# Next batch's loads issued by ScalarE, hand-written lists for the closing rounds, late weights first on SyncE

## The reference, cut to what matters

```python
q = layernorm(x) @ Wq ; k, v = split(layernorm(ctx) @ Wkv)       # ln weights and biases left out
q = q * (1 + scale) + shift
x = x + tanh(g_xattn) * (softmax(q k^T / 8) v) @ Wout
h = gelu(bitlinear(layernorm(x), w1, b1))      # int8 rounding of the rows, ternary weights
x = x + tanh(g_ffn) * bitlinear(h, w2, b2)
```

## Time and profile before

| | us |
|---|---|
| median of 3 runs | 1146.59 (1146.12 to 1147.98) |
| the profiled execution, its own time | 1148.09 |
| its span, first to last instruction | 1146.2 |
| TensorE busy | 1069.4 (93%) |
| ScalarE busy | 974.0 (85%) |
| VectorE busy | 943.3 (82%) |
| GpSimd busy | 776.7 (68%) |
| mean granted TensorE clock | 0.978 of full |

### The profile page before, as it was taken

One profiled execution on the slowest core, in us unless ns is written; L12 is line 12 of the kernel. 1 busy time (PEld: TensorE's weight loads), 2 busy tenths in 40 slices (PEclk: granted clock), 3 DMA queues, 4 the chain that ended last, 5 costly groups with the idle time before them and its releaser, 6 DMA issues.

```text
span 1146.2 us, 32095 instructions
## 1 busy us (share of the span) xinstructions
PE 1069.4 (93%) x11890; PEld 735.4 (64%) x11890; DVE 943.3 (82%) x2108; ACT 974.0 (85%) x1866; POOL 776.7 (68%) x837
## 2 busy tenths in 40 slices
PE   3788999999999999999999999999999999999972
PEld 1455666776676676767666676776677667766650
DVE  3686788888889888888888878888988878988863
ACT  4677789999999979999999979999999979998861
POOL 3466577776767777676777666767777776777631
PEclk9899999999999999999999999999999999999975
DMA  8155745676786656778865776676667676755451
GB/s 273 50 97 91 115 87 108 125 114 113 117 137 108 103 113 124 117 108 125 119 111 110 127 115 104 112 136 101 111 126 114 117 122 111 120 107 103 105 103 30
DMA packets 418840, 129.72 MB, mean 113 GB/s; under 512 B 392480, under 2 KB 417536, under 8 KB 418688
## 3 DMA queue, kind: packets, MB, share of 16 engines
q1 hardware_dynamic: 418688, 127.68, 63.5%
HBM read 26.71 MB, written 3.67 MB: 27 GB/s over the span
## 4 chain that ended last, share of the span: by engine, by line
PE 71%; ACT 9%; DMA 6%; issue 6%; POOL 3%; DVE 3%; POOLq 1%; SPq 0%; DVEq 0%; ACTq 0%
PE work L757 15%; PE work L759 14%; PE work L758 14%; PE ps_s L776 10%; DMA pt<-pn 6%; PE ps_o L757 3%; PE ps_o L759 3%; PE ps_o L758 3%; ACT prob L538 2%; PE work L839 2%; PE work L857 2%; ACT L538 2%; ACT q_f L504 2%; PE work L863 2%; PE work L830 2%
## 5 line engine op out<-in xcount | busy, mean ns | idle before, releaser
L379 POOL TENSOR_TENSOR pn<-prob,pn 112x750 f16<-112x750 f32 x256 | 399.5, 1566 | 123.1 <-ACT pn L548 111.6
L538 ACT ACTIVATE prob<-ps_s,neg_max 112x375 f32<-112x375 f32 x512 | 265.2, 573 | 16.7 <-DVE neg_max L680 13.6
L680 DVE TENSOR_REDUCE neg_max<-ps_s 112x2 f32<-112x750 f32 x256 | 237.4, 928 | 23.6 <-PE ps_s L776 23.5
L757 PE MATMUL ps_o<-v_h,pt 128*128 128x65 f16 (+1 forms) x1536 | 168.3, 195 | 18.3 <-DMA pt<-pn 14.6
L757 PE MATMUL work<-z,wkv_h 128*128 128x375 f16 x512 | 168.6, 329 | 15.2 <-DVE k_l L605 8.1
L461 ACT ACTIVATE k_h<-work 128x375 f16<-128x375 f32 x256 | 121.4, 487 | 61.2 <-PE work L759 55.6
L605 DVE SCALAR_TENSOR_TENSOR k_l<-work,k_h 128x375 f16<-128x375 f32 x256 | 136.3, 540 | 40.7 <-ACT k_h L461 40.5
L758 PE MATMUL ps_o<-v_l,pt 128*128 128x65 f16 (+1 forms) x1536 | 168.0, 193 | 0.0
L759 PE MATMUL ps_o<-v_h,pt 128*128 128x65 f16 (+1 forms) x1536 | 168.0, 194 | 0.0
L759 PE MATMUL work<-z,wkv_l 128*128 128x375 f16 x512 | 167.4, 327 | 0.0
L758 PE MATMUL work<-z,wkv_h 128*128 128x375 f16 x512 | 167.0, 326 | 0.0
(11 more groups left out here) (125 smaller groups left out, 2729.7 us busy)
## 6 DMA issues: line engine op xcount, KB each, us to landing
ctx_in<-in_ctx SPq DMA_DIRECT2D x32, 375.0 KB
pt<-pn SPq DMA_TRANSPOSE x256, 3.5
x_in<-in_x SPq DMA_DIRECT2D x32, 112.0 KB, 3.4
x_res<-in_x SPq DMA_DIRECT2D x28, 128.0 KB, 4.1
out<-y SPq DMA_DIRECT2D x28, 128.0 KB, 2.0
stage<-in_wkv SPq DMA_DIRECT2D x2, 1024.0 KB, 9.6
stage<-in_w SPq DMA_DIRECT2D x2, 1024.0 KB, 11.8
stage<-in_wq SPq DMA_DIRECT2D x1, 1024.0 KB, 9.1
```

Of the source, the lines that this page charges most:

```text
L379: g.tensor_tensor(buf[:, 1, :, 0:SK], prob[:, p % 2], buf[:, 0, :, 0:SK], ALU.subtract).then_inc(p_lo, 1)
L538: i = a.activation(prob[:, p % 2, h, :], ps_s[0:SQ, 2 * (p % 2) + h, 0:SK], ACT.Exp, bias=neg_max[:, 2 * (p % 2) + h:2 * (p % 2) + h + 1])
L680: v.tensor_reduce(neg_max[:, 2 * (p % 2):2 * (p % 2) + 2], ps_s[0:SQ, 2 * (p % 2):2 * (p % 2) + 2, 0:SK], X, ALU.max, negate=True).then_in ...
L757: t_.matmul(dst, sh, mh, start=(n == 0), stop=False)
```

## The change

Four edits. ScalarE issues the loads of the next batch's context and queries right behind `LNW`, after a wait for its own last `LNW` instruction; `LD` and `LX` leave SyncE. The late weights are issued by SyncE at once, ahead of its list. `FIRST` is rewritten for all engines, and a third list, `LAST`, is added for the closing rounds (batches 30 and 31 with tiles 24 to 27). For the last tile, the two DMA transposes become TensorE transposes into PSUM (`XT`, `HT`), from which `XTE` and `HTE` clip. The steady lists of TensorE, ScalarE, VectorE and GpSimd stay as they were. In the lists a tile step carries the number of a batch: 31 is tile 27, 30 is tile 26, 29 is tile 25, 28 is tile 24.

```diff
+LAST["PE"] = [
...
+    ("A3", 31), ("F0", 29), ("WO", 30), ("OO0", 31), ("A4", 31), ("A5", 31), ("A6", 31), ("F2", 28),
+    ("A7", 31), ("OO1", 31), ("F0", 30), ("F1", 30), ("WO", 31), ("F2", 29), ("XT", 31), ("F1", 31),
+    ("F0", 31), ("F2", 30), ("HT", 31), ("F2", 31),
+]
 FIRST["ACT"] = [
+    ("LNW", 0), ("WKH", 0), ("ZF0", 0), ("ZF1", 0), ("WQH", 0), ("KH0", 0), ("WVH", 0), ("WOH", 0),
+    ("KH1", 0), ("KH2", 0), ("ZXF", 0), ("LNW", 1), ("KH3", 0), ("TNH", 0), ("QF0", 0), ("ZF0", 1),
...
+LAST["ACT"] = [
...
+    ("OH1", 30), ("E6", 31), ("PH6", 31), ("VH12", 31), ("E7", 31), ("GE", 29), ("SQ", 29), ("XR", 30),
+    ("OH0", 31), ("OH1", 31), ("HR", 29), ("GE", 30), ("SQ", 30), ("XR", 31), ("HR", 30), ("GE", 31),
 FIRST["DVE"] = [
+    ("BA", 0), ("BB", 0), ("BS", 0), ("WKL", 0), ("BA", 1), ("BB", 1), ("BS", 1), ("WQL", 0),
+    ("KL0", 0), ("WVL", 0), ("KL1", 0), ("KL2", 0), ("AS1", 0), ("KL3", 0), ("AS0", 0), ("KL4", 0),
...
+LAST["DVE"] = [
...
+    ("N0", 31), ("PH5", 31), ("OT1", 30), ("VL11", 31), ("M7", 31), ("N1", 31), ("HE0", 29), ("PH7", 31),
+    ("VL12", 31), ("X1", 30), ("XST", 30), ("N2", 31), ("SC1", 30), ("HTE", 28), ("HMX", 29), ("YE", 28),
+    ("OT0", 31), ("N3", 31), ("SC2", 29), ("XTE", 30), ("OT1", 31), ("HE0", 30), ("HE1", 30), ("X1", 31),
+    ("XST", 31), ("HTE", 29), ("HMX", 30), ("SC1", 31), ("YE", 29), ("SC2", 30), ("XTE", 31), ("HE1", 31),
+    ("HE0", 31), ("HTE", 30), ("HMX", 31), ("YE", 30), ("SC2", 31), ("HTE", 31), ("YE", 31),
+]
 ORDER["SP"] = [
-    ("LX", 4), ("T4", 1), ("T5", 1), ("T6", 1), ("ST", -2), ("T7", 1), ("T0", 2), ("XD", 0),
-    ("HD", -1), ("T1", 2), ("LD", 5), ("T2", 2), ("RS", 1), ("T3", 2),
+    ("T4", 1), ("T5", 1), ("T6", 1), ("ST", -2), ("T7", 1), ("T0", 2), ("XD", 0), ("HD", -1),
+    ("T1", 2), ("T2", 2), ("RS", 1), ("T3", 2),
 ]
-            def load(b):
...
+            def load_late_weights():
+                sp.dma_start(gates[:, 0:1], g_x.partition_broadcast(P)).then_inc(small_in, 16)
...
+            load_late_weights()
             for name, b in sequence("SP"):
...
+            for t in (ident, ident_h):
+                i = g.affine_select(out=t[:], in_=t[:], compare_op=ALU.not_equal, fill=1.0, base=0,
+                                    pattern=[[-1, P]], channel_multiplier=1)
...
                     a.activation(x_n[:], x_in[:], ACT.Identity, bias=ln_nb[0:SQ, TT:TT + 1],
                                  scale=ln_rs[0:SQ, TT:TT + 1]).then_inc(ctx_normed, 1)
+                    if b + 1 < B:
+                        act.wait_ge(ctx_normed, b + 1)
+                        act.dma_start(ctx_in[:], ctx[b + 1].rearrange("(t p) d -> p t d", p=TP)).then_inc(ctx_loaded, 16)
+                        act.dma_start(x_in[:], x[b + 1]).then_inc(x_loaded, 16)
...
+                if name == "XTE" and b == NT - 1:
+                    dve.wait_ge(full[BANK["XT", b]], USE["XT", b])
+                    v.tensor_scalar(xqt[:].rearrange("p c q -> p (c q)"), work[:, BANK["XT", b], :].bitcast(F16)[:, 0:KC * P],
+                                    -QMAX - 1, QMAX, ALU.max, ALU.min).then_inc(evacuated[BANK["XT", b]], 1)
...
+                if name == "HT":
+                    pe.wait_ge(hq_ready, b + 1)
+                    for c in range(FF // P):
+                        i = t_.transpose(wh[:, c * P:(c + 1) * P], hid_q[:, c * P:(c + 1) * P], ident_h[:])
```

More of the change, by code:

```diff
@@ L33 @@
 CAST_ACT = (0, 2, 4, 6)
-ORDER, FIRST = {}, {}
+ORDER, FIRST, LAST = {}, {}, {}
 ORDER["PE"] = [
@@ L115 @@
 FIRST["POOL"] = [
[5 rows of a table removed]
[5 rows of a table added]
+]
+LAST["POOL"] = [
[6 rows of a table added]
 ]
 ORDER["SP"] = [
-    ("LX", 4), ("T4", 1), ("T5", 1), ("T6", 1), ("ST", -2), ("T7", 1), ("T0", 2), ("XD", 0),
-    ("HD", -1), ("T1", 2), ("LD", 5), ("T2", 2), ("RS", 1), ("T3", 2),
+    ("T4", 1), ("T5", 1), ("T6", 1), ("ST", -2), ("T7", 1), ("T0", 2), ("XD", 0), ("HD", -1),
+    ("T1", 2), ("T2", 2), ("RS", 1), ("T3", 2),
 ]
 FIRST["SP"] = [
[6 rows of a table removed]
-]
-START, END = -5, B + 4
[4 rows of a table added]
+]
+LAST["SP"] = [
[5 rows of a table added]
+]
+START, END = -2, B + 4
 TOKEN_STEPS = ("WO", "XT", "HT", "F0", "F1", "F2", "XR", "GE", "SQ", "HR", "X1", "XST", "SC1", "XTE", "HE0", "HE1", "HMX", "SC2",
@@ L139, in sequence @@
 def sequence(engine):
-    done = set(FIRST[engine])
+    done = set(FIRST[engine] + LAST[engine])
     steps = FIRST[engine] + [(name, it + off) for it in range(START, END) for name, off in ORDER[engine]
-                             if 0 <= it + off < B and (name, it + off) not in done]
+                             if 0 <= it + off < B and (name, it + off) not in done] + LAST[engine]
     return [(name, b - b // 8 - 1 if name in TOKEN_STEPS else b) for name, b in steps if b % 8 or name not in TOKEN_STEPS]
@@ L328, in _ @@
                     turn(b, int(name[1]))
-                if name == "XD":
+                if name == "XD" and b < NT - 1:
                     turn_quantised(b)
-                if name == "HD":
+                if name == "HD" and b < NT - 1:
                     turn_hidden(b)
-                if name == "LD":
-                    load(b)
-                if name == "LX" and b > 0:
-                    sp.wait_ge(ctx_normed, b)
-                    sp.dma_start(x_in[:], x[b]).then_inc(x_loaded, 16)
                 if name == "RS":
@@ L350, in _ @@
             g.memset(ident[:], 0.0)
+            g.memset(ident_h[:], 0.0)
             g.memset(ln_mv[:], 1.0)
@@ L353, in _ @@
             pool.drain()
-            g.affine_select(out=ident[:], in_=ident[:], compare_op=ALU.not_equal, fill=1.0, base=0,
-                            pattern=[[-1, P]], channel_multiplier=1).then_inc(consts_ready, 1)
+            for t in (ident, ident_h):
+                i = g.affine_select(out=t[:], in_=t[:], compare_op=ALU.not_equal, fill=1.0, base=0,
+                                    pattern=[[-1, P]], channel_multiplier=1)
+            i.then_inc(consts_ready, 1)
             g.memset(v_h[:, :, :, DH:VW], 1.0)
@@ L719, in step @@
                     scales(x1_rms, b, amax1, x1_c, clip1, inv1, qs1, deq1, 0)
-                if name == "XTE":
+                if name == "XTE" and b == NT - 1:
+                    dve.wait_ge(full[BANK["XT", b]], USE["XT", b])
+                    v.tensor_scalar(xqt[:].rearrange("p c q -> p (c q)"), work[:, BANK["XT", b], :].bitcast(F16)[:, 0:KC * P],
+                                    -QMAX - 1, QMAX, ALU.max, ALU.min).then_inc(evacuated[BANK["XT", b]], 1)
+                if name == "HTE" and b == NT - 1:
+                    dve.wait_ge(full[BANK["HT", b]], USE["HT", b])
+                    v.tensor_scalar(hqt[:].rearrange("p c q -> p (c q)"), work[:, BANK["HT", b], :].bitcast(F16)[:, 0:FF // P * P],
+                                    -QMAX - 1, QMAX, ALU.max, ALU.min).then_inc(evacuated[BANK["HT", b]], 1)
+                if name == "XTE" and b < NT - 1:
                     dve.wait_ge(x_turned, 16 * (b + 1))
                     v.tensor_scalar(xqt[:], xqt_r[:], -QMAX - 1, QMAX, ALU.max, ALU.min).then_inc(x_clipped, 1)
-                if name == "HTE":
+                if name == "HTE" and b < NT - 1:
                     dve.wait_ge(h_turned, 16 * (b + 1))
@@ L798, in job @@
                 w = work[:, bank, :]
+                wh = w.bitcast(F16)
                 if USE[name, b] > 1:
@@ L850, in job @@
                                         for c in range(IC)])
+                if name == "XT":
+                    pe.wait_ge(xq_ready, b + 1)
+                    for c in range(KC):
+                        i = t_.transpose(wh[:, c * P:(c + 1) * P], xq[:, c * P:(c + 1) * P], ident_h[:])
+                if name == "HT":
+                    pe.wait_ge(hq_ready, b + 1)
+                    for c in range(FF // P):
+                        i = t_.transpose(wh[:, c * P:(c + 1) * P], hid_q[:, c * P:(c + 1) * P], ident_h[:])
                 if name in ("F0", "F1"):
@@ L853, in job @@
                         pe.wait_ge(tern_ready[0], 1)
-                    pe.wait_ge(x_clipped, b + 1)
+                    if b == NT - 1:
+                        results(b, ["XT"])
+                    else:
+                        pe.wait_ge(x_clipped, b + 1)
                     c = slice(int(name[1]) * HALF, (int(name[1]) + 1) * HALF)
@@ L860, in job @@
                         pe.wait_ge(tern_ready[1], 1)
-                    pe.wait_ge(h_clipped, b + 1)
+                    if b == NT - 1:
+                        results(b, ["HT"])
+                    else:
+                        pe.wait_ge(h_clipped, b + 1)
                     for c in range(FF // P):
```

20 lines of the change are left out of this document (7 added, 13 removed), and 116 rows, old and new, of the table CAST_ACT.

## The result

The changed kernel takes 1151.95 us (median of 12 runs, 1148.72 to 1154.65); beside it the kernel before took 1147.35 us (12 runs, 1146.12 to 1148.55). The ratio is 1.0038, with a 95% interval of 1.0027 to 1.005: slower, by 4.6 us between the medians, where 14 us less were forecast. The time lies inside the forecast range, and the sign is wrong.

A forecast was written before the change was run, and what follows sets the result against it. TensorE was taken to bound the steady part, with most winnable time at the two ends. 1148.09 us with -6 opening, -12 closing and +4 steady gave 1134.1, or 1132.6 as a median; range 1120 to 1172.

The forecast's parts named there:

- Late weights earlier cost SyncE nothing: Opening: issuing the late weights earlier is free for SyncE, as its first transpose is at 52 us.
- I expect it landed between 18 and 25 us: Opening: the second load, issued by ScalarE near 14 us, lands at 18 to 25 us; opening term -6 us.
- Rival B: Opening gains nothing: loads share the engines with early late weights, landing near 25 us; 1138.6 us; chance 0.14.
- I take 6 us in all: Steady part: gain from transposes of pairs 2 and 3 issued sooner, 6 us, bounds 0 and 9.
- Rounds without a tile have more room: Steady part: rounds without a tile absorb ScalarE's hold more easily; added cost put at 27 x 0.37 = 10 us.
- Rival C: Steady part: ScalarE's issues cost 0.7 to 1.4 us more a round, uncovered; 1145 to 1172 us; chance 0.18.
- A: Whole run: the opening, steady and closing terms add without competing; 1132.6 us, bounds 1120 to 1143; chance 0.48.
- Rival D: Steady part: ScalarE's issues wait for SyncE's transpose issues, 2.5 to 5.1 us a round; 1193 to 1266 us; chance 0.20.
- (b): Closing, after the last `WO`: `XR` and `XQ` no longer behind `HR` and `HQ` of tile 26; 0.3 and 0.6 us.
- (c): Closing: from `XQ`'s end to the clip, two TensorE transposes and a PSUM read replace DMA; 1.5 us won.
- (d): Closing: eight TensorE transposes and a PSUM clip replace the last DMA transpose and its clip; 1.1 us won.
- (a): Closing: tile 26's `HMX` no longer between tile 27's `X1` and `XST`, nor `SC2` before `SC1`; 1.2 and 1.0 us.

The follow-up runs named there:

- E4: Not a run: a code step in ScalarE's list, queued behind the two load issues in the changed kernel; it started 0.09 us after `x_n` ended in the kernel before.
- act_context_alone: The kernel before with only the context's load issued by ScalarE behind its layernorm, SyncE keeping the queries' load: 1144.98 us, ratio 0.9975.
- E5: Not a run: a code step in ScalarE's list, for which TensorE waits before `S7` in rounds without `F0` and `F1`.
- The three issues: The kernel before with both loads issued by ScalarE behind `LNW`, plus a third issue loading the queries into an unread spare tile: 1176.67 us, ratio 1.0254.

## Why the prediction was right or wrong

**The opening: wrong, by its own step.** The steps that failed are "Late weights earlier cost SyncE nothing" and "I expect it landed between 18 and 25 us". SyncE indeed lost nothing. The bytes did: the late weights were in flight beside the second context and made it land at 30.06. That this is the cause, and not the second queue or the new lists, two runs show together: the same issues without the early weights gained 4 to 6 us, and the changed kernel with one wait before the weights took 9.6 less. (The weights first in the kernel before lost 2.2 in the median, but mostly because the context was issued 8 us later.) Rival B named this mechanism, and its sign (a second statistics step after 25 us) is in the trace, but it stopped at "gives nothing"; with the statistics and three weight steps queued behind the load, the price went 1.7 us past nothing. The page that speaks for B (the Trainium skill, DMA: Bandwidth & Descriptors, Issuing engines are not separate DMA queues) says that loads issued by different engines interleave on the same 16 engines. The trace agrees: a queue of its own didn't bring the context in sooner, 16.4 us beside the weights and 8.6 with the weights behind, where on SyncE's queue and ahead of the weights it had taken at most 8.5 (issued at 13.54, read at 22.04).

**The steady part: mechanism right, both terms mis-sized.** Place, waits and releasers came as written: `E4` 1.07 us after `x_n` (forecast 1.0), pair 2's transpose issued 0.03 us after GpSimd (0.99 before), and `KL3`, then `F1`, late.

- What is gained was put at 6 us; `act_context_alone` measured 2.0, within the noise of such a part, with 3.3 of the 5.1 us of wait gone. The step that failed is "I take 6 us in all": it summed the waits as if each microsecond of wait were one of time, and its own sentence, that "The weight loads' wait for `QF` partly takes its place", had been given no share. That row was 7.8 us in the steady stretch and is 11.8 after. In the changed kernel TensorE still waits 4.6 us for transposes over the whole run (14.6 before). The transposes do come sooner, but not by what SyncE's waits and long issues had promised. For pair 2 (medians of batches 4 to 29) the wait and the issue fell from 0.99 and 3.75 us to 0.03 and 1.51, but from the issue's end to landing it took 5.46 instead of 3.24. From its start to landing it is 7.0 in both kernels, and in both a context's load is in flight beside it; only the wait was won. From GpSimd's end to landing pair 2 went from 8.1 to 7.0 us, pair 3 from 8.95 to 8.5 and pair 4 from 6.05 to 4.1.
- What is added was put at 27 x 0.37 = 10 us. By the prediction's own numbers 1.1 - 0.67 is 0.43, and 27 x 0.43 is 11.6. The hold grew by 1.07 + 0.09 = 1.16, less 0.67 is 0.49, and the usual round grew by 0.56. So the mechanism was right there, and nearly the size. The step that failed is "Rounds without a tile have more room": the nine rounds in which a tile's step is missing grew by 6.3 us together, 0.7 each, because TensorE waits there for ScalarE itself (`S7` for `E5`, `Z1` behind `QF`) and has no slack of 0.67. With 7.7 in the fifteen usual rounds and -0.7 in the first two that is the 13.3 measured. The three issues agree: the usual round grew again by at least the hold.

**Rival C** had part of this: a cost of ScalarE beyond the slack. Its price was 0.7 to 1.4 a round more than A; the rows show 0.2 more in the usual round and 0.3 more in the short ones. Its mechanism, longer issues, didn't come: the median issues (0.27 and 0.63) held through the steady part. (28 x 0.7 on top of 1132.6 is 1152, not the 1145 that it names.)

**Rival D didn't come**, at least not in the steady part. In the round shown ScalarE's issues, 467.18 to 468.11, run wholly or in part inside SyncE's transpose issue, 466.58 to 468.08, and are about as long as SyncE's own had been (medians 0.27 and 0.63 for 0.27 and 0.57). Only in the opening, with three weight loads of 1024 KB each queued, did ScalarE's query issue take 1.89 us and end within 0.02 of SyncE's, where it took 0.34 without them; and the context's first issue took 0.55 or 0.56 with and without them. Whether these are such waits or a full queue was not told apart.

**The closing: right in the sum, by luck in part**, 11.0 for 12, and inside the bounds of 6 and 16. The forecast had 6 us up to the end of the last `WO` and 6 behind it; the trace has 9.6 and 1.5. The reordering ahead of `WO` won more than was asked of it, part of it by the clock (1.00 instead of 0.66 in the last 20 us there). Behind it most terms came: (b) was 0.7 for 0.9, (c) 1.8 for 1.5, and (d) 1.9 to the start of the clip, or 1.7 with the longer clip, for 1.1, as clip and transposes at low clock took 0.69 and 1.02 where up to 1.2 and 1.9 had been allowed. But (a) gave 0.3 of 2.2, as `HMX` of tile 26 still ran before `SC1`, at 1126.51, and two losses were in no term: `LAST` puts `HTE` and `YE` of tile 26 between `GE` and `SC2` of tile 27, and from the one to the other it took 5.3 us instead of 3.3; and the last store landed 3.15 us after its issue began instead of 1.7. Most of the gain is the reordering.

**The sum.** -6 -12 +4 became +1.7 -11.0 +13.3 = +4.0 us. The error of 18 us is 7.7 in the opening, 9.3 in the steady part and 1.0 in the closing. Chances of 0.63 for faster rested on A, and A had both of its uncertain terms at the favourable side of a rival that was written down beside it. That the time lies in the range is luck: it is outside A's own bounds, 1120 to 1143, and B and C, which stretch the range, were each right only in part.

## What to carry to other kernels

An engine that issues a load pays its issue time and the wait before it in full once its slack is used, so weigh the hold (here 0.49 against 1.16 us) against the slack of its next reader (0.67) before splitting issues among engines; in the usual round one load fitted, two didn't. Do it for every kind of round: in two of three short rounds there was no such slack, and even one load cost 0.33. Bytes that nobody needs soon are not free when issued early: put them behind the load that the next step waits for, even if the queue that issues them is idle. And when a wait of the bounding engine is removed, ask which second wait ends just behind it before counting it as time.
